# Reordering the score, exponential, mask and value units of a windowed-attention layer's software pipeline

## The chip, the cores and the metric

The kernel runs on all 8 cores of one Trainium2 chip. Each core computes 2 of the 16 sequences and the cores exchange nothing. The metric is the device time in microseconds of the slowest core; smaller is better.

## What is computed

```python
# x: (16, 2048, 1024) fp32; 16 query heads of 64, 2 key/value heads, window 256
q = x @ Wq + bq ; k = x @ Wk + bk ; v = x @ Wv + bv
idx = arange(s)[:, None] + arange(WINDOW)[None, :]      # on k, v padded by 128 at both ends
scores = einsum('bgrsd,bgswd->bgrsw', qg, kp[:, :, idx])
probs = softmax(scores)
out = einsum('bgrsw,bgswd->bgrsd', probs, vp[:, :, idx]) @ Wo + bo
x = layernorm(x + out)
# feed-forward: one complex 512 x 512 matrix, each part unfolded from two small factors
out_real = x_real @ W_real.T - x_imag @ W_imag.T + bias_real
out_imag = x_real @ W_imag.T + x_imag @ W_real.T + bias_imag
x = layernorm(x + concatenate([out_real, out_imag]))
```

## The kernel before, in words

There is no scheduler. `schedule` is run once for each engine and emits that engine's instructions in one fixed order, so the order of the calls in the loop is the order of the work on every engine's queue at once. A wait is written out on a semaphore, and each engine runs its queue in order.

A sequence of 2048 rows is cut into 16 tiles of 128 query rows. Queries, keys and values are projected a quarter (4 tiles) at a time by `emit_qkv`: quarters 0 and 1 ahead of the loop, 2 after iteration k = 5, 3 after k = 9. The loop over k runs 18 iterations for each of the two sequences ("batches" b = 0, 1) of a core. Iteration k works on three tiles: S = k (scores), P = k - 1 (values, output projection, first layernorm) and Q2 = k - 2 (feed-forward, second layernorm). Iterations k = 2 to 15 have all three; k = 1 has no Q2, k = 16 no S, k = 17 only Q2.

A query tile sees three key blocks c = 0, 1, 2 (left, own, right). The units, and the lines that the profile names:

- `sc_unit(b, S, c, pair)` (L509, PE): two score matmuls of 64x512 into two of the three PSUM banks `pSC`. The unit's first matmul takes the bank that the unit before the last one filled, its second the bank of the first matmul of the last unit: so of two score units in a row, the second's last matmul waits for the first's first exponential.
- `exp_unit` (L527, ACT): two exponentials `pSC` -> `EX`, each waiting for both matmuls of the unit. `mask_unit` (L541, POOL): two multiplications of `EX` by a mask, for c = 0 and 2 only.
- `av_unit(b, P, quad)` (L564, PE): 12 matmuls of 128x65 on all three c of one quad into one of two banks `pAV` (quad modulo 2). It waits for the masks and exponentials of its quad, and, for quads 2 and 3, for `normts_unit` of quads 0 and 1 to have emptied the bank. Pair 0 of the scores feeds quads 0 and 1, pair 1 feeds 2 and 3.
- `recip_unit` (L582) and `normts_unit` (L592), DVE: divide by the softmax sum into `attn`.
- `attnT_unit` (L614 PE, L622 DVE), `wo_unit` (L639, L643, PE; half 0 and 1), `ln1_unit` (L682, then the statistics L652 to L662, DVE), `rstd1_unit` (L699, L704, ACT), `x1norm_unit` (L717, DVE).
- `x1t_unit` (L737 PE, L744 DVE), `ffn_unit` (L766, L770, PE; half 0 and 1), `ln2out_unit` (L785, L652 to L662 DVE, L798, L803 ACT, L811 DVE, and the store L819, issued by POOL).

`EX` has 24 slots, 12 for each parity of the tile. The three transposing units share the PSUM tile `pT`, and the projection, `wo_unit` and `ffn_unit` share the banks `pW0` and `pW1`.

Of the kernel before, what the change touches and what calls it, by code (L numbers as in the profile page):

```python
# [18 lines left out]
def build_nc(debug=False):  # L19
# [138 lines left out]
    def schedule(E):  # L158
# [678 lines left out]
        for b in range(NB):  # L837
# [11 lines left out]
                E.c["dc"] += 16  # L849
            for k in range(18):  # L850
                S, P, Q2 = k, k - 1, k - 2
                if 0 <= P < 16:
                    sc_unit(b, P, 2, 0)
                    exp_unit(b, P, 2, 0)
                    mask_unit(b, P, 2, 0)
                    sc_unit(b, P, 2, 1)
                    exp_unit(b, P, 2, 1)
                    mask_unit(b, P, 2, 1)
                if S < 16:
                    sc_unit(b, S, 0, 0)  # L860
                    exp_unit(b, S, 0, 0)
                    sc_unit(b, S, 0, 1)
                    exp_unit(b, S, 0, 1)
                    mask_unit(b, S, 0, 0)
                    mask_unit(b, S, 0, 1)
                if 0 <= Q2 < 16:
                    x1t_unit(b, Q2)
                    ffn_unit(b, Q2, 0)
                if 0 <= P < 16:
                    av_unit(b, P, 0)  # L870
                if S < 16:
                    sc_unit(b, S, 1, 0)
                    exp_unit(b, S, 1, 0)
                if 0 <= P < 16:
                    av_unit(b, P, 1)
                    recip_unit(b, P, 0)
                    recip_unit(b, P, 1)
                    normts_unit(b, P, 0)
                    normts_unit(b, P, 1)
                if S < 16:  # L880
                    sc_unit(b, S, 1, 1)
                    exp_unit(b, S, 1, 1)
                if 0 <= P < 16:
                    av_unit(b, P, 2)
                if 0 <= Q2 < 16:
                    ffn_unit(b, Q2, 1)
                if 0 <= P < 16:
                    av_unit(b, P, 3)
                    recip_unit(b, P, 2)
                    recip_unit(b, P, 3)  # L890
                    normts_unit(b, P, 2)
                    normts_unit(b, P, 3)
                    attnT_unit(b, P)
                if 0 <= Q2 < 16:
                    ln2out_unit(b, Q2)
                if 0 <= P < 16:
                    wo_unit(b, P, 0)
                    wo_unit(b, P, 1)
                    ln1_unit(b, P)
                    rstd1_unit(b, P)  # L900
                    x1norm_unit(b, P)
                if k == 5:
                    emit_qkv(b, 2)
                if k == 9:
                    emit_qkv(b, 3)
                if debug and b == 0 and k == 9:
                    if cur == "g":
                        gps.wait_ge(SEMH["s"], E.res("KT3")["r"][1])
                        gps.wait_ge(SEMH["v"], E.res("VB3")["r"][1])
                        gps.dma_start(dbg["dkt"], KT[:]).then_inc(SEMH["dc"], 16)  # L910
                        gps.dma_start(dbg["dvb"], VB[:]).then_inc(SEMH["dc"], 16)
                    E.c["dc"] += 32
# [89 lines left out]
```

## Time and profile before

| | us |
|---|---|
| time, median of 2 runs | 1571.26 (1567.77 to 1574.75) |
| the profiled execution, its own time | 1568.2 |
| its span, slowest core | 1566.6 |
| spans of the 8 cores | 1555.0 to 1566.6 |
| mean granted TensorE clock, 8 cores | 0.717 to 0.720 |
| busy: PE, DVE, ACT, POOL | 948.9, 510.2, 395.8, 327.7 |

### The profile page before, as it was taken

The numbers are of one execution on the slowest core, as the hardware profiler recorded it, in microseconds if no ns is written. First come the engines' busy times: TensorE is split into PE (matmuls) and PEld (weight loads), VectorE is DVE, ScalarE is ACT, GpSimd is POOL, SyncE is SP. The second block draws the span as 40 slices with busy tenths as digits, with TensorE's granted clock in tenths as the row PEclk, the third lists the DMA queues.
The fourth block names the chain that finished last, engine by engine and source line by source line (L and its number), as shares of the span: only waits on it lengthen the run. The fifth ranks groups of instructions, "written<-read, shape, count | busy, mean of one in ns | idle before, by whom it ended". The sixth has DMA issues, their size and how long they took to land.

```text
span 1566.6 us, 17012 instructions; the slowest of 8 cores (1555.0 to 1566.6 us)
## 1 busy us (share of the span) xinstructions
PE 948.9 (61%) x4568; PEld 370.1 (24%) x4568; DVE 510.2 (33%) x1539; ACT 395.8 (25%) x673; POOL 327.7 (21%) x324
## 2 busy tenths in 40 slices
PE   0076336666666757666664676675767657766663
PEld 0032002222222223222221332222322222222221
DVE  0011442434133331443343103444033331443343
ACT  3332123222222223223210342222322213223210
POOL 0000005222023302223310023222032202223310
PEclk9987555777776678677677776667766667676677
DMA  4520000000200010000001200001000010000000
GB/s 133 162 65 1 0 1 1 14 14 14 67 14 14 14 67 1 14 27 14 15 14 54 81 0 1 14 14 52 30 14 14 14 67 1 14 28 14 14 14 27
DMA packets 15869, 44.51 MB, mean 28 GB/s; under 512 B 3091, under 2 KB 5539, under 8 KB 15782
## 3 DMA queue, kind: packets, MB, share of 16 engines
q0 software_dynamic: 9216, 33.56, 6.0%
q1 hardware_dynamic: 6566, 9.87, 2.2%
q8 instruction: 45, 0.74, 0.2%
q14 instruction: 42, 0.34, 0.1%
HBM read 26.65 MB, written 16.78 MB: 28 GB/s over the span
## 4 chain that ended last, share of the span: by engine, by line
PE 52%; DVE 17%; issue 11%; ACT 10%; DMA 7%; DVEq 1%; POOL 0%; ACTq 0%; SPq 0%; POOLq 0%
PE pW L766 14%; PE pW L639 10%; PE pW L411 8%; ACT EX L527 7%; PE pSC L509 5%; DMA xs<-x 4%; DVE attn L592 4%; PE pAV L564 4%; DVE scr L652 3%; PE pT L737 2%; PE pT L614 2%; PE pW L770 2%; DVE pre L785 2%; PE pW L643 2%; DVE x1T L744 1%
## 5 line engine op out<-in xcount | busy, mean ns | idle before, releaser
L527 ACT ACTIVATE EX<-pSC,expbias 128x512 bf16<-128x512 f32 x384 | 242.3, 682 | 224.8 <-PE pSC L509 222.1
L509 PE MATMUL pSC<-QT,KT 64*128 64x512 bf16 x384 | 154.2, 478 | 147.8 <-ACT EX L527 146.3
L541 POOL TENSOR_TENSOR EX<-EX,maskr_s 128x512 bf16<-128x512 bf16 x128 | 147.5, 1177 | 291.1 <-ACT EX L527 291.1
L639 PE MATMUL pW<-wo_sb,attnT 128*128 128x512 bf16 x512 | 175.9, 505 | 50.9 <-DVE pre L785 48.5
L541 POOL TENSOR_TENSOR EX<-EX,maskl_s 128x512 bf16<-128x512 bf16 x128 | 145.1, 1159 | 157.2 <-ACT EX L527 157.2
L819 POOL DMA_DIRECT2D y<-outst x32 | 19.0, 593 | 615.3 <-DVE outst L811 615.3
L766 PE MATMUL pW<-wrt,x1T 128*128 128x512 bf16 x256 | 114.5, 599 | 36.9 <-DVE x1T L744 36.9
L411 PE MATMUL pW<-XT,wq_sb 128*128 128x512 bf16 x512 | 130.5, 423 | 9.1 <-DVE XT L391 9.1
L582 DVE RECIPROCAL Rrec<-pAV 128x4 f32<-128x4 f32 x128 | 23.4, 183 | 319.9 <-PE pAV L564 314.1
L381 PE MATMUL pT<-identb,x_tm 128*128 128x128 bf16 x256 | 32.4, 307 | 149.1 <-ACT x_tm L371 133.8
L592 DVE TENSOR_SCALAR attn<-pAV,Rrec 128x64 bf16<-128x64 f32 x512 | 110.2, 278 | 14.3 <-DVE attn L592 0.5
L798 ACT ACTIVATE st<-st 128x1 f32<-128x1 f32 x32 | 6.5, 203 | 412.5 <-DVE st L662 412.5
L564 PE MATMUL pAV<-VB,EX 128*128 128x65 bf16 x1536 | 76.0, 204 | 36.3 <-ACT EX L527 29.8
L639 PEld LDWEIGHTS pW<-wo_sb,attnT 128*128 128x128 bf16 x512 | 55.7, 118 | 148.5 <-issue 127.2
L509 PEld LDWEIGHTS pSC<-QT,KT 64*128 64x128 bf16 x384 | 30.0, 96 | 247.4 <-issue 243.6
L652 DVE SCALAR_TENSOR_TENSOR scr<-pre 128x1024 bf16<-128x1024 f32 x64 | 78.4, 1226 | 6.7
L614 PE MATMUL pT<-identb,attn 128*128 128x128 bf16 x256 | 31.0, 297 | 79.9 <-DVE attn L592 79.9
L564 PEld LDWEIGHTS pAV<-VB,EX 128*128 128x128 bf16 x1536 | 60.7, 104 | 73.7 <-issue 73.7
L411 PEld LDWEIGHTS pW<-XT,wq_sb 128*128 128x128 bf16 x512 | 54.2, 107 | 83.6 <-issue 35.6
L420 ACT ACTIVATE QT<-pW,bq_sb 128x512 bf16<-128x512 f32 x64 | 44.0, 687 | 115.0 <-PE pW L411 115.0
L744 DVE COPY x1T<-pT 128x1024 bf16<-128x1024 bf16 x32 | 22.1, 692 | 140.6 <-PE pT L737 140.6
L471 DVE COPY VB<-pT 128x128 bf16<-128x128 bf16 x32 | 7.3, 229 | 184.5 <-PE pT L465 184.5
(81 smaller groups left out, 867.5 us busy)
## 6 DMA issues: line engine op xcount, KB each, us to landing
xs<-x POOLq DMA_DIRECT2D x32, 512.0 KB, 4.7
y<-outst POOLq DMA_DIRECT2D x32, 512.0 KB, 3.0
wstage<-wq SPq DMA_DIRECT2D x4, 512.0 KB, 4.2
xs<-wq SPq DMA_DIRECT2D x4, 512.0 KB, 4.8
wstage<-wo SPq DMA_DIRECT2D x4, 512.0 KB, 4.7
xs<-wo SPq DMA_DIRECT2D x4, 512.0 KB, 4.7
wstage<-wk SPq DMA_DIRECT2D x1, 512.0 KB, 5.4
xs<-wv SPq DMA_DIRECT2D x1, 512.0 KB, 5.1
```

What stands on the lines that cost most here:

```text
L411: i = ten.matmul(pW[bank][:, :], wq_sb[:, c * 1024 + t * 128: c * 1024 + (t + 1) * 128], rhsXT(c), start=(c == 0), stop=(c == 7)) \
L420: i = sca.add(QT[:, parity * 4096 + t * 512: parity * 4096 + (t + 1) * 512], pW[bank][:, :], bq_sb[:, t:t + 1])
L509: i = ten.matmul(pSC[banks[gq]][:, :], lhsT, rhs, start=True, stop=True, tile_position=(rowbase, 0)) if cur == "t" else None
L527: i = sca.activation(EX[:, exi * 512:(exi + 1) * 512], pSC[banks[gq]][:, :], AF.Exp, bias=expbias[:])
L541: i = gps.tensor_mul(EX[:, exi * 512:(exi + 1) * 512], EX[:, exi * 512:(exi + 1) * 512], m[:]) \
L564: i = ten.matmul(pAV[bank][:, hh * 65:(hh + 1) * 65], EX[:, exi * 512 + hh * 128: exi * 512 + (hh + 1) * 128], VB[:, (kb + 1) * 130 + g * ...
L592: i = vec.tensor_scalar(attn[:, ring * 1024 + quadcol[quad] + hh * 64: ring * 1024 + quadcol[quad] + (hh + 1) * 64], ap3(pAV[bank], hh * 6 ...
L614: i = ten.transpose(pT[:, c * 128:(c + 1) * 128], attn[:, ring * 1024 + c * 128: ring * 1024 + (c + 1) * 128], identb[:]) if cur == "t" el ...
L639: ten.matmul(pW[half][:, :], attnT[:, ring * 1024 + c * 128: ring * 1024 + (c + 1) * 128], wo_sb[:, c * 1024 + half * 512: c * 1024 + (hal ...
L652: lambda: vec.scalar_tensor_tensor(scr[:], pre_getter(), 1.0, pre_getter(), ALU.mult, ALU.mult, accum_out=stt[:, c0 + 2:c0 + 3]),
L744: i = vec.tensor_copy(x1T[:, ring * 1024:(ring + 1) * 1024], pT[:, :]) \
L766: ten.matmul(pW[half][:, :], x1T[:, ring * 1024 + c * 128: ring * 1024 + (c + 1) * 128], wsrc[:, wc * 512:(wc + 1) * 512], start=(c == 0), ...
```

## The change

Only the order of the calls in the loop changes. The score, exponential and mask units of key block c = 2 belonged to tile P and stood at the head of the next iteration; they now belong to tile S and stand near the end of its own iteration. `av_unit` of quads 0 and 1 moves ahead of `x1t_unit` and half 0 of the feed-forward, `av_unit` 2 ahead of half 1, and the second score unit of block 1 behind half 1. No instruction is added or removed and none changes its shape. The functions called are those listed above.

```diff
@@ in the loop: for k in range(18): S, P, Q2 = k, k - 1, k - 2
-                if 0 <= P < 16:
-                    sc_unit(b, P, 2, 0)
-                    exp_unit(b, P, 2, 0)
-                    mask_unit(b, P, 2, 0)
-                    sc_unit(b, P, 2, 1)
-                    exp_unit(b, P, 2, 1)
-                    mask_unit(b, P, 2, 1)
                 if S < 16:
                     sc_unit(b, S, 0, 0)
                     exp_unit(b, S, 0, 0)
+                if 0 <= P < 16:
+                    av_unit(b, P, 0)
+                if S < 16:
                     sc_unit(b, S, 0, 1)
                     exp_unit(b, S, 0, 1)
                     mask_unit(b, S, 0, 0)
                     mask_unit(b, S, 0, 1)
+                if 0 <= P < 16:
+                    av_unit(b, P, 1)
                 if 0 <= Q2 < 16:
                     x1t_unit(b, Q2)
                     ffn_unit(b, Q2, 0)
                 if 0 <= P < 16:
-                    av_unit(b, P, 0)
-                if S < 16:
-                    sc_unit(b, S, 1, 0)
-                    exp_unit(b, S, 1, 0)
-                if 0 <= P < 16:
-                    av_unit(b, P, 1)
                     recip_unit(b, P, 0)
                     recip_unit(b, P, 1)
                     normts_unit(b, P, 0)
                     normts_unit(b, P, 1)
                 if S < 16:
-                    sc_unit(b, S, 1, 1)
-                    exp_unit(b, S, 1, 1)
+                    sc_unit(b, S, 1, 0)
+                    exp_unit(b, S, 1, 0)
                 if 0 <= P < 16:
                     av_unit(b, P, 2)
                 if 0 <= Q2 < 16:
                     ffn_unit(b, Q2, 1)
+                if S < 16:
+                    sc_unit(b, S, 1, 1)
+                    exp_unit(b, S, 1, 1)
+                    sc_unit(b, S, 2, 0)
+                    exp_unit(b, S, 2, 0)
+                    mask_unit(b, S, 2, 0)
                 if 0 <= P < 16:
                     av_unit(b, P, 3)
+                if S < 16:
+                    sc_unit(b, S, 2, 1)
+                    exp_unit(b, S, 2, 1)
+                    mask_unit(b, S, 2, 1)
+                if 0 <= P < 16:
                     recip_unit(b, P, 2)
                     recip_unit(b, P, 3)
                     normts_unit(b, P, 2)
                     normts_unit(b, P, 3)
                     attnT_unit(b, P)
```

Behind these lines, unchanged: `ln2out_unit(b, Q2)`, `wo_unit(b, P, 0)`, `wo_unit(b, P, 1)`, `ln1_unit`, `rstd1_unit` and `x1norm_unit` of P, and `emit_qkv` after k = 5 and k = 9.

## Rows read from the trace of the kernel before

**Rows 1.** The page's chain of work that ended last, shares of the span

```profile
PE 52%; DVE 17%; issue 11%; ACT 10%; DMA 7%; DVEq 1%; POOL 0%; ACTq 0%; SPq 0%; POOLq 0%
```

**Rows 2.** Waits: who waited for whom, us in total, times, longest us

```profile
PE pSC L509 <- ACT EX L527: 146.3, 129, 4.5
...
PE pT L614 <- DVE attn L592: 79.9, 32, 2.9
```

**Rows 3.** Timeline of DVE, iteration by iteration: start us, us, instruction, idle before

```profile
644.02 0.69 DVE L744 COPY x1T<-pT 128x1024 bf16<-128x1024 bf16 x1 [4.52 <-PE pT L737]
...
712.21 0.69 DVE L744 COPY x1T<-pT 128x1024 bf16<-128x1024 bf16 x1 [4.52 <-PE pT L737]
```

**Rows 4.** Timeline of all engines, the head of iteration k = 9

```profile
535.90 1.25 ACT L527 ACTIVATE EX<-pSC,expbias 128x512 bf16<-128x512 f32 x2
536.24 0.81 DVE L717 TENSOR_SCALAR x_tm<-pre,st,rstd 128x1024 bf16<-128x1024 f32 x1 [0.93 <-ACT rstd L704]
536.71 1.16 PE L509 MATMUL pSC<-QT,KT 64*128 64x512 bf16 x2 [4.19 <-ACT EX L527]
...
540.36 1.04 PE L737 MATMUL pT<-identb,x_tm 128*128 128x128 bf16 x8
```

**Rows 5.** The same timeline, the middle and the end of iteration k = 8

```profile
512.50 0.64 PE L564 MATMUL pAV<-VB,EX 128*128 128x65 bf16 x12
513.07 0.39 PE L509 MATMUL pSC<-QT,KT 64*128 64x512 bf16 x2
...
513.61 2.62 ACT L527 ACTIVATE EX<-pSC,expbias 128x512 bf16<-128x512 f32 x4 [5.82 <-PE pSC L509]
514.44 0.37 PE L509 MATMUL pSC<-QT,KT 64*128 64x512 bf16 x1 [0.20 <-ACT EX L527]
515.89 0.62 PE L564 MATMUL pAV<-VB,EX 128*128 128x65 bf16 x12 [1.07 <-ACT EX L527]
516.32 1.90 PE L766 MATMUL pW<-wit,x1T 128*128 128x512 bf16 x4
520.07 0.54 PE L564 MATMUL pAV<-VB,EX 128*128 128x65 bf16 x12
523.09 1.01 PE L614 MATMUL pT<-identb,attn 128*128 128x128 bf16 x8 [2.48 <-DVE attn L592]
526.29 1.23 DVE L652 SCALAR_TENSOR_TENSOR scr<-pre 128x1024 bf16<-128x1024 f32 x1
```

**Rows 6.** By stretches: length, busy PE, PEld, DVE, ACT, POOL, granted clock, DMA

```profile
516.30:520.05 3.75, 3.75 (x13) 1.16 (x10) 0.18 (x1) 0.00 (x0) 0.00 (x0) 0.56 0.00 0
...
525.70:529.75 4.05, 4.03 (x9) 1.10 (x9) 2.40 (x8) 0.50 (x2) 0.00 (x0) 0.50 0.02 6
529.75:532.00 2.25, 2.25 (x12) 0.89 (x12) 1.42 (x3) 0.00 (x0) 0.59 (x1) 0.98 0.00 0
532.00:536.70 4.70, 0.52 (x3) 0.04 (x4) 3.08 (x9) 1.21 (x4) 0.00 (x0) 0.99 0.28 112
...
550.20:552.35 2.15, 2.15 (x16) 0.79 (x12) 0.22 (x2) 0.12 (x1) 0.00 (x0) 1.00 0.00 0
```

**Rows 7.** Timeline of iterations k = 0 and 1 of batch 0

```profile
231.95 6.55 POOL L541 TENSOR_TENSOR EX<-EX,maskl_s 128x512 bf16<-128x512 bf16 x4 [124.01 <-ACT EX L527]
232.31 1.99 DVE L337 CAST wit<-wacc 128x2048 bf16<-128x2048 f32 x1
...
238.46 4.47 POOL L541 TENSOR_TENSOR EX<-EX,maskr_s 128x512 bf16<-128x512 bf16 x4
...
243.07 0.82 PE L564 MATMUL pAV<-VB,EX 128*128 128x65 bf16 x12
...
243.82 0.79 PE L509 MATMUL pSC<-QT,KT 64*128 64x512 bf16 x2
```

**Rows 8.** Timeline of iteration k = 16 of batch 0, PE behind ffn half 0

```profile
816.55 0.91 PE L564 MATMUL pAV<-VB,EX 128*128 128x65 bf16 x24
...
819.40 0.52 PE L564 MATMUL pAV<-VB,EX 128*128 128x65 bf16 x12 [1.93 <-DVE attn L592]
```

## Prediction, made before the changed kernel was seen

> **What bounds the kernel now.** The chain of work that ended last comes first: PE holds half of it, and the rest is spread over DVE, issue, ACT and DMA, so no engine is the bound; the order is [rows 1]. The list of waits names PE's largest idle time inside the loop: score matmuls waiting for exponentials, 129 times, and the transposes of `attn` waiting for the division, 32 times [rows 2]. The DVE timeline gives the length of an iteration: three x1T copies lie at 644.02, (678.08) and 712.21 us, so one takes 34.1 us [rows 3]. There are 28 such iterations (k = 2 to 15 in two batches).
>
> The head shows the first stall. After the projection PE starts the score units of the iteration and stops for 4.19 us, since the exponentials stand on ACT's queue behind `rstd1_unit`, which waits for the layernorm of the tile before. At 535.90 ACT is free, and three more score units run at the pace of exponentials, 1.57 us each. Only at 540.36 do the x1 transposes start, though x1 was normalised at 537.05 [rows 4].
>
> The middle: between the end of the feed-forward's half 0 (512.50) and half 1 (516.32) lie 3.82 us for two value units, two score units and a wait of 1.07 us. The profile puts that wait down to ACT; in the code the unit also waits for the division of quad 0. Then come value unit 3 at 520.07 and the transposes 3.02 us later, 2.48 of them idle [rows 5].
>
> The stretches show the clock. Half 1 of the feed-forward took 3.75 us at 0.56, and 2.15 us at 1.00 one iteration later. The projection's half 0 ran at 0.50 (4.05 us), half 1 at 0.98 (2.25 us). After the sparse stretch between the two feed-forward halves the clock fell; after a dense one it rose [rows 6].
>
> **The change, part by part.** Times in one iteration; nothing is added, all is moved.
>
> *Head.* PE's order is now score unit 0.0, value 0, score 0.1, value 1, x1 transposes. The wait for `rstd1_unit` stays: 0.1's second matmul needs a bank that an exponential behind `rstd1_unit` empties, so it still starts at 536.71. Value 0 runs inside the stall and costs nothing there. The matmul takes about 0.6 (half of 1.16) and value 1 takes 0.6 (0.64 in [rows 5]), so the transposes start at 537.9 instead of 540.36: 2.45 us saved. The floor is x1 at 537.05 and a release of 0.2, so at most 3.1; the least is 1.85 if value 1 took twice as long [rows 4, 5].
>
> *Middle.* Between the two halves only score 1.0 and value 2 are left. From 512.50 a value unit leads to the next instruction in 0.57, and the two score matmuls take 0.39: 0.96 where 3.82 was. Value 2's bank is emptied by divisions that now run under half 0 (behind value 3 the same work takes 2.48 us; half 0 and score 1.0 take at least 2.5). I take 2.85 us saved; the least is 1.8, if the wait of 1.07 stays in another place [rows 5, 6].
>
> *End.* Behind half 1 stand score 1.1, score 2.0, value 3, score 2.1. The same pair of units side by side is seen from 513.07: first matmul to the exponential 0.54, to the second unit's last matmul 1.37, that one 0.37. So value 3 starts 1.7 us later than now. Score 2.1 then lies in the 2.48 us in which PE waits for the division: its last matmul needs the first exponential of 2.0, the third of four in a row (513.61 + 3 x 0.655 = 515.58, so 2.7 after the first matmul), and ends 3.1 after it, where the transposes start at 1.7 + 3.0 = 4.7. It costs nothing; without this cover it would cost 0.4. Cost of the end: 1.7, at most 2.2 [rows 5].
>
> *What is moved past other queues.* ACT gets six exponentials ahead of `ln2out_unit`'s two small ones; the last ends 513.61 + 6 x 0.655 - 513.07 = 4.5 us after half 1, ahead of the transposes. On POOL the four masks of block 2 now stand ahead of the store and of the loads that follow it after k = 5 and 9. They need 4.47 us [rows 7] from 2.5 on, so to about 7.1, while the store waits for a DVE result that comes behind L652, which starts 3.2 us after the transposes (523.09, 526.29), at 7.9 [rows 5]. Stores and loads are not delayed, and the value units now find masks that have been ready since the iteration before.
>
> *Sum at the clock as it is.* 2.45 + 2.85 - 1.7 = 3.6 us; 28 times, 101 us. At k = 16 there are no scores: the middle there spends 0.91 on two value units and 1.93 waiting for the division [rows 8], of which about 2.6 goes, twice, 5 us. At k = 1 the same eight score units lead to the first value unit's masks, and I take nothing. Together 106.
>
> *The clock.* Half 1 now follows half 0 after 1.0 us instead of 3.8, as the projection's half 1 follows its half 0, and that one runs at 0.98. The sparse stretch ahead of the fall is gone. Warm, it takes 1.6 us less (3.75 to 2.15) [rows 6]. Two of the 28 already run warm (k = 5 and the one in the row). The head still has 3.6 us of idling, so half 0 stays slow, and a rise that comes late will fall into half 1: I take 1.2 of the 1.6 for 26 iterations, 31 us. Bounds: nothing, and 1.6 for half 1 with another 1.0 from earlier rises in both half 0s (DVE's own chain holds back more there), 70 us.
>
> The sum is 137 us. The profiled execution took 1568.2, so 1431; it lies 3 us under the median, so 1434 on the scale of the medians.
>
> **A rule against the change.** DVE and POOL slow each other in this trace: four masks took 6.55 us while DVE cast `wacc`, and 4.47 without [rows 7]. The last mask of block 2 ends by my sum at 7.1, and DVE's L652, which reads two SBUF operands, starts at 7.9: a margin of 0.8 us. The Trainium skill (SBUF — State Buffer on-chip working memory, section "Who interferes with whom") says that a VectorE instruction with two SBUF inputs and a GpSimd instruction that reads SBUF exclude each other, and that the later one blocks for the whole of the other. That agrees with the 6.55. By the rows there is no meeting and the sum stays; if the masks come 0.8 us later, L652 waits for up to one mask, 1.1 us, on the chain: 28 times, 31 us, 1465.
>
> **The rivals.**
> 1. *The clock follows the new order no better than the old.* The order's own 106 us alone: 1465. For it: rise and fall repeat with the iteration and half 1 is slow in 26 of 28. Against: every dense half 1 of the projection runs fast.
> 2. *Masks meet L652*, as above: 1465. For it the margin of 0.8; against it that both ends hang on the same score pace.
> 3. *The fast part moves.* Half 1 of the feed-forward is fast, and the projection's half 1 becomes slow, as its half 0 is: 4.05 for 2.25, 1.8 x 28 = 50 us back, 1484.
> 4. *The head gives nothing*, since x1 transposes still wait for something behind `rstd1_unit`: 2.45 x 28 = 69 back, 1503. Against it: x1 is ready at 537.05.
> 5. *The other side: PE stays at 1.2 GHz through the whole iteration.* The work is spread more evenly, and no stretch may be dense enough. Place: everything that is fast now. Price per iteration: projection half 1 1.8, four value units 0.82 for 0.54, 1.1, three score units 0.79 for 0.39, 1.2: 4.1 against the 3.6 saved [rows 5 to 7]. That is 28 x 0.5 = 14 more, 5 less at k = 16: 1580, slower than before. It decides where the clock is 0.5 in nearly all stretches; a third of the fast time kept makes it faster again. Against it: dense halves of 4 us stay as they are, and the clock rose behind them.
> 6. *The change does not do what it says.* The scores of block 2 could still pace PE at the end as they did at the head (no cover by the wait for the division): 0.4 to 1.6 more, 1445 to 1479. This is inside the range.
>
> **Chances.** The forecast with its clock gain: 0.58, on its own 1400 to 1455. Rival 1 0.19, rival 2 0.07, rival 3 0.04, rival 4 0.03, rival 5 0.03, rival 6 0.06. The low bound is 1568 - 106 - 70 = 1392, 1395 on the medians' scale. The high bound takes in rivals 1, 2 and 6, 1465 and 1479, with a little for the edges: 1482. Left out are rivals 3 to 5, 0.10, and what lies below. Over 2% (31 us, about what a measurement of this kernel tells from no change): faster in all cases but rival 5 and an unforeseen loss, 0.93; within 2% 0.05; slower by more 0.02.
>
> **What would show it.** The iteration goes from 34.1 to 29.3 us: x1T copies follow each other at that distance (30.5 without the clock). The x1 transposes start about 1 us after L717 ends. L766's half 1 starts 1.0 us behind half 0, and its eight matmuls take about 2.2. The wait of the scores for exponentials falls from 146 us: one of 3.6 at the head of each iteration and two short ones. The wait at L614 stays an idle of about 1.5 behind score 2.1. L652's mean stays 1.23. A mean granted clock under 0.70 would speak for rivals 3 and 5, an L652 above 1.3 for rival 2, a gap from L717 to L737 above 2 us for rival 4.

## The result, and the profile after

The changed kernel took 1426.45 us (median of 9 runs, 1423.60 to 1431.26) against 1571.44 us (8 runs): a ratio of 0.908 with a 95% interval of 0.907 to 0.910, so 145 us or 9.2% faster. The forecast was 1434. One execution here (1456.87 us), and one of four in gap_wait, warm_head, all_three, rstd_late_warm and all_warm below, was 1 to 3% longer at a lower clock on one die: the ratios leave these out, while the medians of the experiments hold them and are up to 2.5 us higher for it. The profiled execution took 1426.94 us, its slowest core's span 1425.4; the one before took 1568.2, so the two traces differ by 141 us.

The head of the page after: the span, then busy time, share of the span and instructions of each engine.

```profile
span 1425.4 us, 17008 instructions; the slowest of 8 cores (1415.0 to 1425.4 us)
PE 870.0 (61%) x4568; PEld 364.9 (26%) x4568; DVE 504.0 (35%) x1539; ACT 396.0 (28%) x673; POOL 328.4 (23%) x324
```

DVE, ACT and POOL are as busy as before to within some 6 us. PE executed the same instructions in 79 us less (948.9 before), and 62 us of its idle time are gone. The mean granted clock of the 8 cores rose from 0.717 to 0.720 to 0.731 to 0.740. With the two levels 0.5 and 1.0 that is little in the mean and much in time: 2 x (1 - 0.718) x 1566 = 883 us at 1.2 GHz before, 2 x (1 - 0.735) x 1425 = 755 us after.

From the list of waits after (engine, line waited for: total us, times, longest):

```profile
PE pSC L509 <- ACT EX L527: 115.4, 66, 4.0
```

Scores wait 66 times instead of 129, and 31 us less in all [rows 2]; what is left is the head's wait of up to 4.0 us. The groups of instructions (count | busy us, mean ns | idle us before) show where the clock rose:

```profile
L766 PE MATMUL pW<-wit,x1T 128*128 128x512 bf16 x128 | 36.8, 414 | 0.0
L639 PE MATMUL pW<-wo_sb,attnT 128*128 128x512 bf16 x512 | 178.3, 511 | 50.9 <-DVE pre L785 48.5 <-DVE attnT L622 2.4
L652 DVE SCALAR_TENSOR_TENSOR scr<-pre 128x1024 bf16<-128x1024 f32 x64 | 78.4, 1226 | 6.7
```

`wit` is read by half 1 of the feed-forward alone; its matmuls took 593 ns on average before. The projection (L639) stayed near where it was (505), and L652 too: no mask stood in its way.

One iteration after (k = 9), lines of PE, DVE and POOL, by start time and duration, with the idle time before and its releaser in brackets:

```profile
502.48 0.58 PE L509 MATMUL pSC<-QT,KT 64*128 64x512 bf16 x1 [3.62 <-ACT EX L527]
503.65 1.04 PE L737 MATMUL pT<-identb,x_tm 128*128 128x128 bf16 x8
505.82 1.86 PE L766 MATMUL pW<-wrt,x1T 128*128 128x512 bf16 x4 [1.12 <-DVE Rrec L582]
509.86 0.61 PE L509 MATMUL pSC<-QT,KT 64*128 64x512 bf16 x2
510.40 0.84 PE L564 MATMUL pAV<-VB,EX 128*128 128x65 bf16 x12
511.05 1.40 PE L766 MATMUL pW<-wit,x1T 128*128 128x512 bf16 x4
512.29 1.03 PE L766 MATMUL pW<-wrt,x1T 128*128 128x512 bf16 x4
513.57 0.60 PE L509 MATMUL pSC<-QT,KT 64*128 64x512 bf16 x3
515.49 0.53 PE L564 MATMUL pAV<-VB,EX 128*128 128x65 bf16 x12 [0.18 <-ACT EX L527]
516.30 4.48 POOL L541 TENSOR_TENSOR EX<-EX,maskr_s 128x512 bf16<-128x512 bf16 x4 [9.14 <-ACT EX L527]
518.49 0.91 PE L614 MATMUL pT<-identb,attn 128*128 128x128 bf16 x8 [1.82 <-DVE attn L592]
521.02 3.57 PE L639 MATMUL pW<-wo_sb,attnT 128*128 128x512 bf16 x8 [1.62 <-DVE pre L785]
521.59 1.23 DVE L652 SCALAR_TENSOR_TENSOR scr<-pre 128x1024 bf16<-128x1024 f32 x1
```

- Head: the stall for the bank that stands behind `rstd1_unit` is still there (3.62 us). The x1 transposes start 1.17 us after the late score matmul; before it was 3.65 [rows 4].
- Middle: from the end of half 0 (509.86) to half 1 (511.05) there are 1.19 us, where 3.82 us lay before [rows 5]. In 18 of the 28 iterations it is shorter still, 0.7 to 0.8 us, and the mean is 0.9. Its eight matmuls and bias take 2.5 us, and the first four show the clock rising in the middle of it: 1.40 us, then 1.03.
- End: value 3 starts 1.92 us after half 1, with 0.18 us of idle time right before it. The transposes come 3.0 us after that, as before.
- The last mask of block 2 ends at 516.30 + 4.48 = 520.78, and L652 starts at 521.59: a margin of 0.81 us.

The windows after, of this iteration's half 0, half 1, projection half 0 and half 1 (stretch: length, busy us of each engine, granted clock, DMA share and GB/s):

```profile
505.82:509.86 4.04, 4.04 (x10) 1.09 (x11) 1.72 (x8) 0.00 (x0) 1.33 (x2) 0.50 0.00 0
511.05:513.57 2.52, 2.52 (x15) 0.88 (x12) 0.18 (x1) 0.83 (x2) 0.00 (x0) 0.85 0.00 0
521.02:525.20 4.18, 4.18 (x10) 1.22 (x11) 2.73 (x9) 0.50 (x2) 0.00 (x0) 0.50 0.00 0
525.20:528.00 2.80, 2.26 (x9) 0.68 (x7) 1.44 (x4) 0.00 (x0) 1.65 (x3) 0.95 0.22 89
```

Of the four halves three were slow before; two are now, both behind idle time on PE: half 0 behind the head's stall, the projection's half 0 behind the division and L785.

From one set of x1 transposes to the next, over the 26 distances of a trace without a quarter of projections between them, it is 28.8 us on average instead of 33.6. Without k = 16 it is 29.0 instead of 33.9 (typically 34.1; now often 28.2 and 29.9 in turn), across a quarter 66.7 instead of 69.8, and at k = 16 26.2 instead of 30.5. 24 x 4.89 + 4 x 3.1 + 2 x 4.25 = 138, against 141 between the traces.

Summed over k = 2 to 15 of both batches, 28 iterations, the parts changed like this (us; negative is time saved; short matmuls within the first three also follow the clock):

| part of the iteration, on PE | forecast | measured |
|---|---|---|
| head, from the projection to the x1 transposes | -69 | -62 |
| middle, between the feed-forward's halves | -80 | -82 |
| end, from half 1 to the projection | +48 | +58 |
| half 1 of the feed-forward | -31 | -38 |
| half 0, and both halves of the projection | 0 | -6 |
| k = 16, twice | -5 | -8.5 |

### The profile page after: what moved, and what is told of

Same layout as the page of the kernel before. It is cut to its first block, busy times and chain, and to the rows that moved or that the text cites. A ratio compares the mean times of both kernels' runs of the same rounds, so it can differ in the third digit from the quotient of the medians.

```text
span 1425.4 us, 17008 instructions; the slowest of 8 cores (1415.0 to 1425.4 us)
## 1 busy us (share of the span) xinstructions
PE 870.0 (61%) x4568; PEld 364.9 (26%) x4568; DVE 504.0 (35%) x1539; ACT 396.0 (28%) x673; POOL 328.4 (23%) x324
## 4 chain that ended last, share of the span: by engine, by line
PE 53%; DVE 18%; issue 12%; DMA 7%; ACT 7%; DVEq 1%; SPq 0%; POOL 0%; ACTq 0%; POOLq 0%
PE pW L766 12%; PE pW L639 11%; PE pW L411 9%; PE pAV L564 4%; DMA xs<-x 4%; DVE attn L592 4%; PE pSC L509 3%; ACT EX L527 3%; DVE scr L652 3%; PE pT L614 2%; PE pT L737 2%; PE pW L770 2%; DVE pre L785 2%; PE pW L643 2%; DVE pre L682 1%
## 5 line engine op out<-in xcount | busy, mean ns | idle before, releaser
L541 POOL TENSOR_TENSOR EX<-EX,maskl_s 128x512 bf16<-128x512 bf16 x128 | 149.2, 1191 | 426.1 <-ACT EX L527 426.1
L639 PE MATMUL pW<-wo_sb,attnT 128*128 128x512 bf16 x512 | 178.3, 511 | 50.9 <-DVE pre L785 48.5
L541 POOL TENSOR_TENSOR EX<-EX,maskr_s 128x512 bf16<-128x512 bf16 x128 | 143.2, 1150 | 245.2 <-ACT EX L527 245.2
L509 PE MATMUL pSC<-QT,KT 64*128 64x512 bf16 x384 | 115.7, 437 | 116.6 <-ACT EX L527 115.4
L766 PE MATMUL pW<-wrt,x1T 128*128 128x512 bf16 x256 | 92.5, 500 | 36.7 <-DVE Rrec L582 34.4
L582 DVE RECIPROCAL Rrec<-pAV 128x4 f32<-128x4 f32 x128 | 19.6, 173 | 251.0 <-PE pAV L564 251.0
L639 PEld LDWEIGHTS pW<-wo_sb,attnT 128*128 128x128 bf16 x512 | 57.1, 121 | 150.3 <-issue 132.0
L564 PE MATMUL pAV<-VB,EX 128*128 128x65 bf16 x1536 | 82.1, 212 | 15.3 <-ACT EX L527 11.3
L564 PEld LDWEIGHTS pAV<-VB,EX 128*128 128x128 bf16 x1536 | 66.7, 109 | 56.9 <-issue 56.9
L652 DVE SCALAR_TENSOR_TENSOR scr<-pre 128x1024 bf16<-128x1024 f32 x64 | 78.4, 1226 | 6.7
L509 PEld LDWEIGHTS pSC<-QT,KT 64*128 64x128 bf16 x384 | 26.6, 95 | 178.3 <-issue 171.5
L391 DVE COPY XT<-pT 128x1024 bf16<-128x1024 bf16 x32 | 22.1, 692 | 133.0 <-PE pT L381 133.0
```

The lines of the kernel that those rows point to most:

```text
L509: i = ten.matmul(pSC[banks[gq]][:, :], lhsT, rhs, start=True, stop=True, tile_position=(rowbase, 0)) if cur == "t" else None
L541: i = gps.tensor_mul(EX[:, exi * 512:(exi + 1) * 512], EX[:, exi * 512:(exi + 1) * 512], m[:]) \
L564: i = ten.matmul(pAV[bank][:, hh * 65:(hh + 1) * 65], EX[:, exi * 512 + hh * 128: exi * 512 + (hh + 1) * 128], VB[:, (kb + 1) * 130 + g * ...
L639: ten.matmul(pW[half][:, :], attnT[:, ring * 1024 + c * 128: ring * 1024 + (c + 1) * 128], wo_sb[:, c * 1024 + half * 512: c * 1024 + (hal ...
L652: lambda: vec.scalar_tensor_tensor(scr[:], pre_getter(), 1.0, pre_getter(), ALU.mult, ALU.mult, accum_out=stt[:, c0 + 2:c0 + 3]),
L766: ten.matmul(pW[half][:, :], x1T[:, ring * 1024 + c * 128: ring * 1024 + (c + 1) * 128], wsrc[:, wc * 512:(wc + 1) * 512], start=(c == 0), ...
```

## The experiments

The kernel before took 1568 to 1570 us beside each group of runs; ratios are against it. Changes of less than about 5 us between two kernels are not read as differences. Edits are against the changed kernel where nothing else is said, with `...` for lines left out; "iteration" is the mean of the 26 distances of the x1 transposes, as above.

**block2_only.** Only the units of block 2 move; value units 0 and 1 and the score units of block 1 keep the places that they had before. The edit is against the kernel before.

```diff
             for k in range(18):
                 S, P, Q2 = k, k - 1, k - 2
-                if 0 <= P < 16:
-                    sc_unit(b, P, 2, 0)
-                    exp_unit(b, P, 2, 0)
-                    mask_unit(b, P, 2, 0)
-                    sc_unit(b, P, 2, 1)
-                    exp_unit(b, P, 2, 1)
-                    mask_unit(b, P, 2, 1)
...
                 if 0 <= Q2 < 16:
                     ffn_unit(b, Q2, 1)
+                if S < 16:
+                    sc_unit(b, S, 2, 0)
+                    exp_unit(b, S, 2, 0)
+                    mask_unit(b, S, 2, 0)
                 if 0 <= P < 16:
                     av_unit(b, P, 3)
+                if S < 16:
+                    sc_unit(b, S, 2, 1)
+                    exp_unit(b, S, 2, 1)
+                    mask_unit(b, S, 2, 1)
+                if 0 <= P < 16:
                     recip_unit(b, P, 2)
```

> Only the score, exponential and mask units of key block 2 move into their own iteration (one ahead of value unit 3, one behind it); value units 0 and 1, score 1.0 and 1.1 stay between the halves of the feed-forward, as before. Theory (each stall is paid where it stands): the x1 transposes start 0.25 us after L717 ends, which saves 3.05 us of the 34.1; the end costs 0.4; the middle stays at 3.8 us and half 1 of the feed-forward stays slow (3.75 us). 28 x 2.65 = 74 us under before: 1497 us. Rival A (all of the gain is block 2 leaving the head, the rest is hidden): about 1426, as the full change. Rival B (any denser order also speeds up the clock): half 1 at 2.2 to 2.5 us, 1455.

Measured 1483.12 us, ratio 0.945 [0.943, 0.946]; iteration 30.9, typically 30.7. Its timeline of PE:

```profile
645.41 1.01 PE L737 MATMUL pT<-identb,x_tm 128*128 128x128 bf16 x8
651.43 0.54 PE L564 MATMUL pAV<-VB,EX 128*128 128x65 bf16 x12
654.70 0.82 PE L564 MATMUL pAV<-VB,EX 128*128 128x65 bf16 x12 [1.04 <-ACT EX L527]
657.02 1.54 PE L766 MATMUL pW<-wrt,x1T 128*128 128x512 bf16 x4
```

The transposes start with x1 (L717 ends at 645.16), the middle keeps its 3.9 us (651.43 to 655.33) and half 1 stays slow (3.5 us). So 87 of the 145 us belong to taking block 2 out of the head, and 57 to the value units and score 1.1, with the clock of half 1 among them. I expected 1497: 14 us of the first part were not in that sum. Most of them are clock: over the 28 iterations the four halves took 12 us less in all, each of them a little, though none became fast.

**values_back.** Value units 0 and 1 behind half 0, all else as changed.

```diff
                     exp_unit(b, S, 0, 0)
-                if 0 <= P < 16:
-                    av_unit(b, P, 0)
-                if S < 16:
                     sc_unit(b, S, 0, 1)
...
-                if 0 <= P < 16:
-                    av_unit(b, P, 1)
                 if 0 <= Q2 < 16:
                     x1t_unit(b, Q2)
                     ffn_unit(b, Q2, 0)
                 if 0 <= P < 16:
+                    av_unit(b, P, 0)
+                    av_unit(b, P, 1)
                     recip_unit(b, P, 0)
```

> The changed kernel with value units 0 and 1 put back behind half 0 of the feed-forward (both ahead of score 1.0). Theory: the head gets 0.6 us shorter, since value 1 leaves it; the gap between the halves grows from 1.2 us to 3.2, as at k = 16 of before, with a wait for the division in it: +1.4 us, 28 times, 1465 us, if half 1 stays fast. If the sparse gap makes the clock fall, as in the kernel before, half 1 takes 3.75 us for 2.3 and the time is about 1505. Rival (place of the value units does not count): 1426.

Measured 1508.14 us, ratio 0.960 [0.958, 0.962]; iteration 31.7: most 30.9 or 31.1, some 33.1. The time is that of the case "half 1 slow", but half 1 is fast in 20 of the 28 iterations (mean of the `wit` matmuls 452 ns). PE and then the windows of the same stretch, the gap between the halves and half 1:

```profile
660.98 0.52 PE L564 MATMUL pAV<-VB,EX 128*128 128x65 bf16 x12 [1.61 <-ACT EX L527]
661.34 0.81 PE L766 MATMUL pW<-wit,x1T 128*128 128x512 bf16 x3
662.21 1.03 PE L766 MATMUL pW<-wrt,x1T 128*128 128x512 bf16 x4
```
```profile
658.06:661.34 3.28, 1.67 (x39) 1.35 (x39) 2.08 (x10) 1.26 (x2) 0.00 (x0) 0.97 0.00 0
661.34:663.50 2.16, 2.11 (x16) 0.80 (x14) 0.18 (x1) 0.00 (x0) 0.00 (x0) 1.00 0.00 0
```

Between the halves PE was busy for 1.67 of 3.28 us (1.9 at most, since the first of half 1's matmuls is missing in this record), where the kernel before had it busy for 2.55 of 3.82 us (window 512.50 to 516.32, clock 0.95). The gap is the emptier one of the two, and yet half 1 ran at 2.4 GHz here and at 1.2 there. That a sparse gap ahead of it makes half 1 slow is therefore not true in general. The 82 us over the changed kernel are about these: the gap is 2.5 us longer on average, so 70 over 28 iterations; 10 are the 8 slow half 1s, 12 a slower projection (530 for 511 ns) and 9 lie at k = 16, while the head is 17 shorter.

**gap_wait.** The gap alone: PE waits for the exponentials of score unit 1.0 ahead of half 1, nothing is moved.

```diff
                 if 0 <= Q2 < 16:
+                    if cur == "t" and S < 16:
+                        E.wait(E.ev[f"exp_{S % 2}_1_1"])
                     ffn_unit(b, Q2, 1)
```

> The changed kernel, where half 1 of the feed-forward also waits for both exponentials of score 1.0. Nothing else moves. In the trace of after these end at 511.9, half 1 starts at 511.05, so PE idles 1.0 us more in each of 28 iterations. If the clock does not mind: +1.0 x 28 = 28 us, 1454. If the clock follows the density of this place: half 1 gets slower by up to 1.5 us as well, up to 1496. If another wait behind it takes the loss up: 1426 to 1435.

Measured 1473.76 us, ratio 0.938 [0.935, 0.940], 47 us over the changed kernel; iteration 30.5, typically 30.6.

```profile
PE pW L766 <- ACT EX L527: 37.3, 28, 1.6
497.65 1.02 PE L766 MATMUL pW<-wit,x1T 128*128 128x512 bf16 x4 [1.34 <-ACT EX L527]
L639 PE MATMUL pW<-wo_sb,attnT 128*128 128x512 bf16 x512 | 188.9, 535 | 50.9 <-DVE pre L785 48.5 <-DVE attnT L622 2.4
```

(A wait, a line of PE's timeline and a group of instructions.) The added wait is 37 us. Half 1 starts at the fast clock behind an idle of 1.34 us, as in 24 of the 28 iterations; what became slower is the projection: 512 matmuls at 24 ns more each are 12 us. So the idle time costs itself and about 10 us of clock, in another place than the one where it stands.

**masks_late.** The masks of block 0 are emitted behind those of block 2, which puts them under L652. The same multiplications, later on POOL.

```diff
                     exp_unit(b, S, 0, 1)
-                    mask_unit(b, S, 0, 0)
-                    mask_unit(b, S, 0, 1)
...
                     mask_unit(b, S, 2, 1)
+                    mask_unit(b, S, 0, 0)
+                    mask_unit(b, S, 0, 1)
```

> The changed kernel with the four masks of block 0 emitted behind those of block 2, so that eight masks run in a row from about 516.3 to 525.3 in the iteration shown, across DVE's L652 (at 521.6) and L811 (at 524.9). They are needed only in the next iteration. Theory (the two engines exclude each other, the later waits for a whole instruction): L652 of the second layernorm takes up to 1.14 us more, L811 and the masks a share, +0.6 to 2.0 us an iteration on the chain, 1443 to 1482. Rival (no such price, the 6.55 us for four masks had another cause): 1426, with L652's mean at 1.23.

Measured 1451.34 us, ratio 0.924 [0.923, 0.926], 25 us over the changed kernel; iteration 29.2. POOL's and DVE's timeline, then two groups:

```profile
525.79 5.45 POOL L541 TENSOR_TENSOR EX<-EX,maskl_s 128x512 bf16<-128x512 bf16 x4
529.15 1.00 DVE L662 TENSOR_TENSOR st<-st 128x1 f32<-128x1 f32 x1
L652 DVE SCALAR_TENSOR_TENSOR scr<-pre 128x1024 bf16<-128x1024 f32 x64 | 93.2, 1457 | 6.7
L662 DVE TENSOR_TENSOR st<-st 128x1 f32<-128x1 f32 x64 | 32.7, 511 | 7.1 <-DVE st L660 0.5
```

Rival 2's mechanism is real. L652 costs 15 us more in all (16 of 64 are slower, up to 2.25 us), L662, which works on one column, 22 us more (160 ns before, up to 1.01 us here), and the four masks take 5.45 us instead of 4.5. The Trainium skill ("SBUF — State Buffer", section "Who interferes with whom") calls it an exclusive lock of the port pair that the two engines share; the rows agree, and they add that an instruction on one column is held up too.

**rstd_late.** The stall at the head is made by `rstd1_unit` ahead of the first exponentials on ACT's queue. Here it and `x1norm_unit` are emitted in the next iteration, behind the exponentials of block 0, except where a quarter of projections follows (k = 5 and 9).

```diff
                     mask_unit(b, S, 0, 1)
+                if 0 <= Q2 < 16:
+                    if k not in (6, 10):
+                        rstd1_unit(b, Q2)
+                        x1norm_unit(b, Q2)
...
                     ln1_unit(b, P)
-                    rstd1_unit(b, P)
-                    x1norm_unit(b, P)
+                    if k in (5, 9):
+                        rstd1_unit(b, P)
+                        x1norm_unit(b, P)
```

> The changed kernel with rstd1_unit and x1norm_unit of P emitted in the head of the next iteration, behind the exponentials of score 0.1 (not at k = 5 and 9, where a projection follows). ACT then takes the four exponentials of the head before the two small ones, so score 0.1 no longer waits for the layernorm; both score units and both value units fit into the 4.7 us before x1 is ready. Theory: the wait of 3.6 us of L509 on L527 is replaced by a wait of the x1 transposes for L717; they start 0.25 us after L717 instead of 0.84: 0.6 us less in 24 iterations, 14 us, about 1412. Rival (ACT's exponentials now delay L699, since the fourth ends late): no gain, 1426 to 1440.

Measured 1444.89 us, ratio 0.921 [0.919, 0.922]: 18 us slower than the changed kernel, where I expected 14 us faster.

```profile
506.33 5.21 POOL L541 TENSOR_TENSOR EX<-EX,maskl_s 128x512 bf16<-128x512 bf16 x4 [1.10 <-ACT EX L527]
508.34 1.01 DVE L662 TENSOR_TENSOR st<-st 128x1 f32<-128x1 f32 x1
510.36 1.74 DVE L717 TENSOR_SCALAR x_tm<-pre,st,rstd 128x1024 bf16<-128x1024 f32 x1 [1.01 <-ACT rstd L704]
512.35 1.01 PE L737 MATMUL pT<-identb,x_tm 128*128 128x128 bf16 x8 [4.93 <-DVE x_tm L717]
```

The stall of the scores is gone (32.7 us of waiting left in all, 0.8 at most), and PE waits 124.9 us for x1 in its place. But the exponentials now come early, so the masks of block 0 do too, and they fall on the statistics and on L717, which takes 1.74 us instead of 0.81 here and is slow in 12 of 32 cases. That is the same exclusion, in a place where I had not looked for it; x1 comes later than without the edit (from the projection to the x1 transposes it is 6.8 us on average, 6.0 in the changed kernel).

**rstd_late_score** adds score 1.0 to that head, ahead of the x1 transposes, to fill it. The edit is against rstd_late.

```diff
                     av_unit(b, P, 1)
+                if S < 16:
+                    sc_unit(b, S, 1, 0)
+                    exp_unit(b, S, 1, 0)
                 if 0 <= Q2 < 16:
                     x1t_unit(b, Q2)
...
-                if S < 16:
-                    sc_unit(b, S, 1, 0)
-                    exp_unit(b, S, 1, 0)
-                if 0 <= P < 16:
                     av_unit(b, P, 2)
```

> As rstd_late, and score 1.0 also in the head, ahead of the x1 transposes (its exponentials behind the small ones). Theory: the gap between the halves of the feed-forward loses score 1.0, 1.2 us to 0.6, and the head pays nothing since PE idles there: 0.5 us more in 28 iterations, 1398. Rival: its second matmul must wait for the first exponential of 0.1 and the clock falls sooner: 1412 or more.

Measured 1439.73 us, ratio 0.918 [0.916, 0.920]: at most 5 us better than rstd_late, and still behind the changed kernel; PE still waits 112 us in all for x1.

**rstd_late_clean.** rstd_late, and the masks of block 0 wait on POOL until x1 is written (they are emitted behind value 1 now, which changes nothing for POOL's order). The edit is against rstd_late.

```diff
                     exp_unit(b, S, 0, 1)
-                    mask_unit(b, S, 0, 0)
-                    mask_unit(b, S, 0, 1)
...
                     av_unit(b, P, 1)
                 if 0 <= Q2 < 16:
+                    if S < 16:
+                        if cur == "g" and k not in (6, 10):
+                            E.wait(E.ev[f"x1ev_{Q2 % 2}"])
+                if S < 16:
+                    mask_unit(b, S, 0, 0)
+                    mask_unit(b, S, 0, 1)
+                if 0 <= Q2 < 16:
                     x1t_unit(b, Q2)
```

> rstd_late with one more wait: the four masks of block 0 start only when x1norm_unit has ended (not at k = 6 and 10, where it ended before a projection). Theory: in rstd_late these masks ran across L662 (1.01 us for 0.16) and L717 (1.74 for 0.81), which cost more than the order gave. Without the meeting L662 and L717 are back at 0.16 and 0.81, 1.8 us less in 24 iterations: 1445 - 43 = 1402, under the changed kernel's 1426. Rival (the loss of rstd_late came from the lower clock behind a longer idle time, 5 us in one piece for 3.6): 1430 to 1445.

Measured 1401.61 us, ratio 0.893 [0.892, 0.895], iteration 27.8: 43 us less than rstd_late, 25 us less than the changed kernel, and no work added.

```profile
620.42 0.16 DVE L662 TENSOR_TENSOR st<-st 128x1 f32<-128x1 f32 x1
621.51 0.81 DVE L717 TENSOR_SCALAR x_tm<-pre,st,rstd 128x1024 bf16<-128x1024 f32 x1 [0.93 <-ACT rstd L704]
622.54 4.46 POOL L541 TENSOR_TENSOR EX<-EX,maskl_s 128x512 bf16<-128x512 bf16 x4 [6.38 <-DVE x_tm L717]
622.61 0.86 PE L737 MATMUL pT<-identb,x_tm 128*128 128x128 bf16 x8 [2.85 <-DVE x_tm L717]
```

The durations are back at 0.16 and 0.81, and the masks at 4.46. PE still waits 2.85 us for x1 (88 us in all instead of 124.9), and the transposes behind that wait take 0.86 us (0.61 at the fast clock, below).

**warm_head.** Is it the idle time at the head that makes half 0 slow? The changed kernel, with 12 matmuls in the stall whose results nobody reads (added work; nothing is left out), in k = 2 to 15.

```diff
                     av_unit(b, P, 0)
+                if 2 <= k < 16 and cur == "t":
+                    E.wait(E.res("avb1")["f"])
+                    for j in range(12):
+                        ten.matmul(pAV[1][:, :], wo_sb[:, j * 128:(j + 1) * 128],
+                                   wo_sb[:, j * 512:(j + 1) * 512], start=True, stop=True)
                 if S < 16:
                     sc_unit(b, S, 0, 1)
```

> The changed kernel with 12 matmuls of 128x512 on weights added in each head (k = 2 to 15) between value 0 and score 0.1, in the time in which PE idles for 3.6 us. They write a value bank that value 1 starts afresh; nothing reads them. 12 x 0.216 = 2.6 us at full clock. Theory (the idle stretch of the head is what makes half 0 of the feed-forward slow): half 0 takes 2.2 us instead of 4.05, 1.9 us less, minus nothing for the matmuls; the x1 transposes and score 0.1 get faster too: up to 28 x 2.1 = 59 us, 1368. Rival (the clock falls all the same, because the head's scores, values and the 1.1 us of waiting for the x1T copy are sparse): 1426. Rival (the matmuls run at the low clock, 5.1 us, and push the head back by 1.5): 1468.

Measured 1392.17 us (1379.07 to 1405.37), ratio 0.885 [0.880, 0.889], 34 us less than the changed kernel; granted clock 0.767 to 0.787.

```profile
640.92 2.75 PE L860 MATMUL pAV<-wo_sb 128*128 128x512 bf16 x12
647.85 1.02 PE L766 MATMUL pW<-wrt,x1T 128*128 128x512 bf16 x4 [1.12 <-DVE Rrec L582]
648.71 1.03 PE L766 MATMUL pW<-witn,x1T 128*128 128x512 bf16 x4
```

Yes: half 0 takes 2.1 us instead of 4.0, in 21 of the 28 iterations of the slowest core and in 24 to 27 on six others. On the slowest core the 28 half 0s take 38 us less and the stretch ahead of them (faster transposes) 12 less; a slower projection takes 17 back, and k = 6 and 10, which have no stall to fill, 14.

**all_three.** rstd_late_score and warm_head together.

> rstd_late_score and warm_head together: the sum of both gains if they are independent, about 1340. If the 12 matmuls now delay score 0.1 and with it the four exponentials ahead of the layernorm's small ones, that delay (up to 2.6 us, as x1 waits for L717) is paid: about 1390 to 1430.

Measured 1470.85 us, ratio 0.938 [0.936, 0.939]: slower than either.

```profile
639.59 2.75 PE L860 MATMUL pAV<-wo_sb 128*128 128x512 bf16 x12
644.81 1.65 DVE L717 TENSOR_SCALAR x_tm<-pre,st,rstd 128x1024 bf16<-128x1024 f32 x1 [1.50 <-ACT rstd L704]
646.71 0.92 PE L737 MATMUL pT<-identb,x_tm 128*128 128x128 bf16 x8 [2.68 <-DVE x_tm L717]
```

With the stall gone (the waits for exponentials are short in rstd_late_score) the 12 matmuls stand ahead of score 0.1 on PE's queue and delay it; the exponentials and, on ACT behind them, the reciprocal root come late, L717 meets the masks (1.65 us; 24 of 32 are slow, 12 of 32 in rstd_late), and PE idles 2.68 us behind the useless work instead of doing it there.

**rstd_late_warm.** rstd_late_clean, with the 12 matmuls behind value 1, where its 2.85 us of idling are (`pSC[spare]`, the bank that the next score unit fills first; not at k = 6 and 10). The edit is against rstd_late_clean.

```diff
                     av_unit(b, P, 1)
+                if 2 <= k < 16 and k not in (6, 10) and cur == "t":
+                    spare = (2 * scu_ctr[0]) % 3
+                    E.wait(E.res(f"pSC{spare}")["f"])
+                    for j in range(12):
+                        ten.matmul(pSC[spare][:, :], wo_sb[:, j * 128:(j + 1) * 128],
+                                   wo_sb[:, j * 512:(j + 1) * 512], start=True, stop=True)
...
                     x1t_unit(b, Q2)
```

> rstd_late_clean with the 12 matmuls of warm_head, put behind value 1, directly ahead of the x1 transposes, into a free score bank. PE is then busy until about 0.7 us before x1 is ready. Theory: the gains of both add up, rstd_late_clean's 24 us under the changed kernel and warm_head's 34: about 1365; half 0 at 2.2 us. Rival: the x1 transposes still wait for L717, the clock falls all the same: 1402.

Measured 1353.18 us (1351.06 to 1380.80), ratio 0.862 [0.861, 0.864]; clock 0.785 to 0.795, iteration 26.6. 48 us less than rstd_late_clean.

```profile
628.00 2.75 PE L870 MATMUL pSC<-wo_sb 128*128 128x512 bf16 x12
630.99 0.61 PE L737 MATMUL pT<-identb,x_tm 128*128 128x128 bf16 x8 [0.24 <-DVE x_tm L717]
632.71 1.02 PE L766 MATMUL pW<-wrt,x1T 128*128 128x512 bf16 x4 [1.12 <-DVE Rrec L582]
635.54 1.02 PE L766 MATMUL pW<-wit,x1T 128*128 128x512 bf16 x4
```

Both halves of the feed-forward are fast here (half 0 in 25 of the 28 iterations), and the added work delays nothing: 0.24 us of waiting is left in front of the transposes.

**warm_two** is warm_head (without k = 6 and 10) with 7 such matmuls ahead of the `attn` transposes and 5 behind them; **all_warm** is rstd_late_warm with the same 12. Each block of the edit stands under `if 2 <= k < 16` on PE and waits for its bank first.

```diff
...
+                    for j in range(7):
+                        ten.matmul(pSC[spare][:, :], wo_sb[:, j * 128:(j + 1) * 128],
+                                   wo_sb[:, j * 512:(j + 1) * 512], start=True, stop=True)
...
                     attnT_unit(b, P)
...
+                    for j in range(5):
+                        ten.matmul(pSC[spare][:, :], wo_sb[:, j * 128:(j + 1) * 128],
+                                   wo_sb[:, j * 512:(j + 1) * 512], start=True, stop=True)
```

> warm_head without its 12 matmuls at k = 6 and 10 (no idle time there), and with 7 such matmuls ahead of the transposes of attn and 5 behind them, in each iteration k = 2 to 15. They fill most of 1.9 and 1.6 us of idling with work at full clock. Theory (what is idle before a dense stretch makes the stretch slow): the transposes take 0.61 us for 1.01 and the projection's half 0 2.2 for 4.05, of which DVE's chain lets through about 0.8: 1.2 us x 28 = 34, and 4 x 2 us from k = 6 and 10: 1392 - 42 = 1350. Rival (the clock is already low there and the matmuls run at half speed, 3.0 and 2.1 us): the transposes start 1.2 us later and the projection 0.6: 1440.

> rstd_late_warm with the 7 and 5 matmuls of warm_two: if all gains are independent, 1365 - 34 = about 1330. If the matmuls ahead of the transposes of attn run slowly, 1400 or more.

Measured 1389.30 us, ratio 0.887 [0.885, 0.888], and 1351.46 us, ratio 0.860 [0.857, 0.863]: 3 and 2 us less than their bases, neither read as a difference. The clock rose all the same (0.807 to 0.813, and 0.831 to 0.843). PE in warm_two:

```profile
618.04 0.37 PE L509 MATMUL pSC<-QT,KT 64*128 64x512 bf16 x1 [1.88 <-ACT EX L527]
621.17 1.48 PE L766 MATMUL pW<-wrt,x1T 128*128 128x512 bf16 x3 [1.50 <-DVE Rrec L582]
635.70 1.89 PE L639 MATMUL pW<-wo_sb,attnT 128*128 128x512 bf16 x8 [0.54 <-DVE pre L785]
```

The projection's half 0 takes 1.89 us instead of 3.57, as intended. But L682 can start only behind L811 on DVE's queue, so the earlier projection ends in a longer idle at the head (1.88 us behind the added matmuls, 1.03 in warm_head), and half 0 of the feed-forward is slow again in nearly every iteration. In all_warm half 0 is slow in 13 of 28. A faster PE in that place waits for DVE; this is read from the rows, and no run tests it.

## Why the prediction was right

The mechanism held: the three places changed as forecast, and half 1 of the feed-forward became fast. That 137 and 138 agree so closely is in part luck: the order gave 85 us where the sum had 101 without k = 16, the clock gave 44 where it had 31, and k = 16 8.5 for 5.

- **Head, 2.45 us.** Held in the iteration shown, where the transposes start 1.17 us after the late score matmul (the sum had 1.2). The stall itself stayed. From the projection's end to the transposes the mean fell from 8.2 to 6.0, so 2.2 over all iterations.
- **Middle, 2.85 us.** Measured 2.9 on average. In the iteration shown the gap is 1.19 us, not 0.96, because the two scores and value 2 ran at 1.2 GHz (0.61 and 0.84); in others they run fast and it is 0.7. The wait of 1.07, which might have stayed, is gone.
- **End, 1.7 us.** Measured 1.92 in the iteration shown and 2.1 on average, within the bound of 2.2 but 10 us too small a cost in all. In the sum value 3 followed the late score matmul at once; in the row it stands behind 0.18 us of idle time. The profile puts that down to an exponential, though value 3 needs none of this iteration's: its cause is not shown. Score 2.1 lay in the idle time and cost nothing.
- **k = 16, 2.6 us.** Measured 4.25. The gap gave 2.85 and the clock of half 1 1.6 (2.2 us for 3.8), which I had not counted there; the projection's half 1 took 0.65 more.
- **Clock, 1.2 us of 1.6.** The size was on the low side: half 1 gave 38 us in all instead of 31 and was faster in all 26 iterations in which it had been slow, and the `wit` matmuls fell from 593 to 414 ns. The reason given for it, that the sparse stretch between the halves is what makes half 1 slow, holds only in part. In values_back and gap_wait idle time stood ahead of half 1 and it ran fast; there, other parts were slower. What the runs show is that where in the iteration the slow parts lie depends on the whole iteration, not on the stretch just before. In this order and in block2_only less idle time came with a faster clock, but I could have been wrong about the place, and in another order about the size.
- **Cover.** L652 stayed at 1.23 us with a margin of 0.81 us, where 0.8 was worked out. That masks_late lost 25 us shows that a meeting costs; rival 2 was priced at 31. The 6.55 us that the prediction took as agreeing with the rule for two SBUF inputs stood beside a cast, which reads one: it showed that the engines slow each other, and it is masks_late that shows it for L652.
- **The wait of the scores.** A forecast on its size was loose: 115 us are left of 146, because the stall at the head is almost all of it.
- **The other rivals.** Rival 1 (1465) did not happen here; block2_only comes nearest to it, where half 1 stayed slow (3.6 us) and the mean clock lay between (0.726 to 0.734). Rival 3 did not either in this kernel (projection 511 for 505 ns), but it did in gap_wait, at 12 us instead of 50. Rivals 4, 5 and 6 did not: the head gave its share, the clock rose, and score 2.1 was covered.

The traces differ by 141 us and the sum had 137. The other 4 us between 1434 and 1426 are that the trace before lay 3 us under its median, and the one after does not.

Left open: block2_only, gap_wait and all_three, three different orders, all typically take 30.6 or 30.7 us an iteration, and most iterations of values_back 30.9 or 31.1. What holds them there no run tells: the coincidence may be the clock's rise and fall falling in step with the iteration, or chance. Nor was a version tried in which DVE's chain (L811 ahead of L682) is shortened, which warm_two points to as the next limit.

## What to carry to other kernels

Price each stall where it stands and ask what is queued behind it: here two small layernorm instructions ahead of exponentials stopped the matmuls 28 times, and emitting them later, with the masks held back, turned the stall into a shorter wait and gave 25 us. Before moving work to an earlier or later place on GpSimd, lay its new times beside VectorE's chain; freeing an engine can put its masks on top of a one-column instruction that everything waits for. Idle time on TensorE can be paid twice, as waiting and as a slower clock for matmuls elsewhere in the loop, so work of any kind inside a stall can gain time, as long as nothing on the path stands behind it in the queue.

## What the runs showed of the hardware that was not expected

- A VectorE instruction on 128x1 numbers took 1.00 us instead of 0.16 because a mask was running on GpSimd, and the normalisation of 128x1024 numbers took 1.74 instead of 0.81, though only one of its operands is a large SBUF tile.
- Twelve matmuls whose results nobody reads made the kernel 34 us faster in one order (1426 to 1392) and 48 us in another (1402 to 1353). They themselves took 2.75 us for 12, 0.23 each, which is the pace of the fast stretches (1.02 for 4 in half 0): the clock was at 2.4 GHz when the stall began, and in the kernel without them it had fallen by its end (the score matmul ahead of the stall takes 0.39 us in both kernels; the late one, behind it, 0.58 in the changed kernel and 0.37 with the added work). The Trainium skill ("TensorE: Matmul & The Clock Gate", section "HAM oscillation — how this bites in real kernels") describes a clock that goes up and down between bursts of matmuls; the traces agree: within one iteration of the changed kernel the windows above stand at 0.50, 0.85, 0.50 and 0.95.
- A higher mean clock is not a shorter time: all_three ran at 0.761 to 0.769 and took 1471 us, rstd_late_clean at 0.740 to 0.748 and took 1402.
